# Where a second layer's hyperbolic half-steps enter, and how one formula is dealt over steps

## The chip, the cores and the metric

The kernel runs on one core of a Trainium2 chip. The metric is the time of one execution on the device in microseconds (us). The compute engines are TensorE (PE; its weight loads are a row of their own, PEld), VectorE (DVE), ScalarE (ACT) and GpSimd (POOL); SP issues most of the DMAs. Each engine works through its own queue in order, and the queues meet only at semaphores.

## The reference, cut to what matters

Two transformer layers over x of shape (4, 1024, 128), each an adaptive layer norm, an attention, a second norm and a mixture of experts. The change touches the attention of the second one ("layer 1"). It has 16 causal heads of width 8 in three groups: 6 plain, 4 hyperbolic, 6 with normalised queries and keys. The plain and normalised ones are `softmax(q k^T * scale + causal)`. The hyperbolic ones compute for each pair of positions

```
inner  = q k^T - tq * tk            # tq, tk = sqrt(1/curv + sum of squares)
arg    = max(-curv * inner, 1 + 1e-7)
dis    = sqrt(1/curv) * arccosh(arg)
scores = 1 / (eps + dis) + causal   # then softmax over keys, times v
```

## The kernel before, in words

The batches go one after another (`b` = 0 to 3), and each passes through the attention and the experts of both layers. In an attention, four heads are a *unit*. The scores are kept transposed, keys on partitions: a unit has `NS` = 12 steps, one for each chunk of 512 queries and each block of 128 keys that it sees (4 for chunk 0, 8 for chunk 1). The widths of the steps are 512, 384, 256, 128 and then five times 512, 384, 256, 128 columns a head.

Layer 1 has three standard units, so 36 standard steps, and one hyperbolic unit (`HYP_UNIT` = 3), whose 12 steps are cut into 24 *halves* of two heads (`HYP_HALVES`). Half k belongs to step k // 2. All engines walk through the same *positions* p = 0, 1, 2, ... Position p holds standard step p, and the halves enter one a position from `HYP_AT` = 2 on: half k is at position k + 2. Its work is spread over four positions (p its entry):

- p: TensorE forms the products (`hyp_scores`, L717), behind everything else of its position.
- p + 1: VectorE forms the argument and its square (`hyp_arg`, L1344 and L1349); ScalarE takes the square root by logarithm and exponential (`hyp_root`, L983 and L984); GpSimd adds root and argument (L1624).
- p + 2: ScalarE runs the rest of the score (`hyp_score`, L989, L992, L995); VectorE adds the negated maxima (`hyp_shift`, L1357).
- p + 3: ScalarE's exponential (`hyp_exp`, L1000); GpSimd's causal cut; TensorE's product with the values (`hyp_values`, L772).

In each position ScalarE first does the two exponentials of the standard step (`std_exp`, L1011), then `hyp_exp`, `hyp_score` and `hyp_root` of three different halves. VectorE does the outputs that are due, `hyp_arg`, the first half of its side jobs, `hyp_shift`, the second half of them.

Score products, standard and hyperbolic, share two pairs of PSUM banks in turn (`take_banks`, with the order written out in `JOBS`): each waits until the one two before it has been read.

Softmax needs row maxima before the scores. They are worked out ahead by *side jobs* (`side_plan`): a `piece` is a product of queries and keys in the other orientation (L628, with the causal mask added by L631) in one of two side banks, reduced by VectorE (L1284). `maxima` gathers the pieces of a unit, `max` transposes the result (L635, L637) and SP sends it on as a row. For the hyperbolic unit a maximum goes through the same formula as a score first. This is done for each chunk of queries alone, by turns on VectorE and ScalarE (L1242 to L1250, L970 to L978, `hyp_max`), and the row is spread through DRAM (`spread_hyp_maxima`). Chunk 0's is done ahead of position 0. Chunk 1's pieces lie in positions 0 to 4, the whole formula in position 4, the row in 6. The pieces of unit 1 lie in 6 to 9, those of unit 2 in 13 to 21. Other side jobs are `turn` (an output is transposed and divided) and, near the end, the first norm of the next batch.

Of the kernel before, what the change touches and what calls it, by code (L numbers as in the profile page):

```python
# [9 lines left out]
NT = N // P  # L10
# [76 lines left out]
HYP_AT = 2  # L87
HYP_HALVES = 2 * NS

# [5 lines left out]
POSITIONS = (UNITS * NS, max(3 * NS, HYP_AT + HYP_HALVES + 3) + 1)  # L95
# [7 lines left out]
def score_jobs(l):  # L103

    steps = STD_UNITS[l] * NS
    jobs = [(False, 0, 0), (False, 0, 1)]
    for p in range(POSITIONS[l]):
        if p + 1 < steps:
            jobs += [(False, p + 1, 0), (False, p + 1, 1)]
        if l and 0 <= p - HYP_AT < HYP_HALVES:  # L110
            jobs.append((True, p - HYP_AT, (p - HYP_AT) % 2))
    return jobs
# [16 lines left out]
def side_plan(l, more):  # L129
# [47 lines left out]
    for p in sorted(plan):  # L177
        items = []
        for kind, what in plan[p]:
            on_pe = kind not in ("maxima", "stats0", "norm0")  # L180
# [58 lines left out]
def adaln_kernel(nc, ins, out):  # L239
    with ExitStack() as ctx:  # L240
# [300 lines left out]
        def tensor_program(pe, b):  # L541
# [18 lines left out]
            def attention(l):  # L560
# [229 lines left out]
                for p in range(POSITIONS[l] + 1):  # L790
# [5 lines left out]
                    if l and 0 <= p - HYP_AT - 3 < HYP_HALVES:  # L796
                        hyp_values(p - HYP_AT - 3)
                    for x in extra:
                        side_job(*x)
                    if l and 0 <= p - HYP_AT < HYP_HALVES:  # L800
                        hyp_scores(p - HYP_AT)
# [94 lines left out]
        def scalar_program(act, b):  # L896
# [47 lines left out]
            def attention(l):  # L944
# [21 lines left out]
                def hyp_max(c):  # L966
# [4 lines left out]
                    nc.scalar.activation(z, z, ACT.Exp, scale=0.5).then_inc(hyp_s, 1)  # L971
                    act.wait_ge(hyp_mx, 2 * c + 2)
# [42 lines left out]
                if l:  # L1015
                    hyp_max(0)
                for p in range(POSITIONS[l]):
                    if p < steps:
                        std_exp(p)
                    if l:  # L1020
                        k = p - HYP_AT
                        if 0 <= k - 3 < HYP_HALVES:
                            hyp_exp(k - 3)
                        if 0 <= k - 2 < HYP_HALVES:
                            hyp_score(k - 2)
                        if 0 <= k - 1 < HYP_HALVES:
                            hyp_root(k - 1)
                        for c in range(NC):
                            if ("maxima", None, (HYP_UNIT, (c,))) in SIDE[l, more][p]:
                                hyp_max(c)  # L1030
# [58 lines left out]
        def vector_program(dve, b):  # L1089
# [120 lines left out]
            def attention(l):  # L1210
# [6 lines left out]
                def maxima(u, chunks):  # L1217
# [21 lines left out]
                    if is_hyp(l, u):  # L1239

                        c = chunks[0]
# [3 lines left out]
                        dve.wait_ge(hyp_s, 2 * c + 1)  # L1245
# [678 lines left out]
```

## Time and profile before

| | us |
|---|---|
| median of 3 runs | 2766.61 (2758.28 to 2769.98) |
| the profiled execution | 2764.56 |
| its span, first to last instruction | 2762.6 |
| TensorE busy | 2252.7 (82%) |
| VectorE busy | 1553.4 (56%) |
| ScalarE busy | 1380.8 (50%) |
| GpSimd busy | 660.7 (24%) |

The clock that TensorE was granted had a mean of 0.81 of full speed. Layer 1's attention of batch 0 lies between about 410 and 655 us of the span; the other three batches follow at distances of some 665 us. Times in rows count from the span's start. A *step* in the text on ScalarE is the time from one standard step's first exponential to the next one's; step 0 of batch 0 begins at 413.76.

### The profile page before, as it was taken

To read this page: it belongs to the slowest core of one execution; us is meant where nothing else is said; L and a number is where in the kernel's file an instruction comes from. 1 tells how busy PE (TensorE), PEld (TensorE's weight loads), DVE (VectorE), ACT (ScalarE), POOL (GpSimd) and SP (SyncE) were. 2 spreads that over 40 slices of the span, in tenths; PEclk is the share of its full clock that TensorE was granted. 3 is DMA by queue.
4 is the path that set the end of the run, shared out by engine and by line. 5 is a ranking of instruction groups with operands and counts; after the bars stand their busy time and mean duration, and the time that the engine had idled before them with its cause. 6 is when DMAs were issued, how large, how long until landed. Compare 5 with 4: busy or idle time off the path is not lost. (4 is left out here: it accounts for less than half of the span.)

```text
span 2762.6 us, 30066 instructions
## 1 busy us (share of the span) xinstructions
PE 2252.7 (82%) x10649; PEld 861.1 (31%) x10649; DVE 1553.4 (56%) x3429; ACT 1380.8 (50%) x1963; POOL 660.7 (24%) x639
## 2 busy tenths in 40 slices
PE   3899867778999896777998987768799998677789
PEld 1222432224433242222443234122343324322234
DVE  2564466666555256675655526566655534666542
ACT  1145426894234532898324452489522454268932
POOL 1012202332422210333331120133242111023324
PEclk9599965568999995667999987566799999655689
DMA  5200230001500023100430012210061002300012
GB/s 140 53 19 2 73 81 31 18 1 48 142 23 19 2 77 92 33 2 1 121 89 23 2 37 79 55 33 1 12 151 43 19 1 77 77 31 18 1 43 88
DMA packets 67845, 128.31 MB, mean 46 GB/s; under 512 B 11396, under 2 KB 24836, under 8 KB 63076
## 3 DMA queue, kind: packets, MB, share of 16 engines
q1 hardware_dynamic: 67696, 126.40, 17.2%
q8 instruction: 84, 1.38, 0.2%
q14 instruction: 65, 0.53, 0.1%
HBM read 109.99 MB, written 15.20 MB: 45 GB/s over the span
## 5 line engine op out<-in xcount | busy, mean ns | idle before, releaser
L1284 DVE TENSOR_REDUCE mx<-ps 128x1 f32<-128x512 f32 (+3 forms) x1248 | 641.5, 553 | 461.1 <-PE ps L631 335.9
L1011 ACT ACTIVATE pr<-ps 128x1024 f32<-128x1024 f32 (+3 forms) x672 | 515.9, 804 | 457.6 <-PE ps L701 455.2
L628 PE MATMUL ps<-kop,qop 72*128 72x512 bf16 (+6 forms) x1248 | 455.7, 388 | 142.1 <-DVE mx L1284 103.9
L701 PE MATMUL ps<-qop,kop 75*128 75x512 bf16 (+7 forms) x1344 | 419.6, 379 | 92.3 <-DVE wb L1344 32.7
L1571 POOL TENSOR_SCALAR_AFFINE_SELECT pr<-pr 128x512 f32<-128x512 f32 x224 | 149.5, 668 | 951.6 <-ACT pr L1011 950.6
L747 PE MATMUL ps<-pr,vt 128*32 128x512 f32 (+3 forms) x2688 | 360.4, 615 | 7.2 <-POOL pr L1571 6.1
L1068 ACT ACTIVATE pr<-ps 128x512 f32<-128x512 f32 x224 | 133.8, 597 | 344.1 <-PE ps L854 280.5
L628 PEld LDWEIGHTS ps<-kop,qop 72*128 72x128 bf16 (+1 forms) x1248 | 124.6, 103 | 551.0 <-DVE mx L1284 329.4
L701 PEld LDWEIGHTS ps<-qop,kop 75*128 75x128 bf16 (+1 forms) x1344 | 125.1, 107 | 328.6 <-ACT pr L1011 127.2
L631 PE MATMUL ps<-maskqk,identb 128*128 128x128 bf16 x832 | 202.3, 251 | 0.0
L864 PE MATMUL ps<-pr,w_down 128*128 128x512 f32 x384 | 197.7, 600 | 3.1 <-POOL pr L1562 3.1
L851 PE MATMUL ps<-hT,w_gate 128*128 128x512 f32 x384 | 196.1, 592 | 0.2 <-DVE on L1509 0.2
L754 PE MATMUL ps<-pr,ones 128*32 128x512 f32 (+3 forms) x1536 | 167.3, 508 | 0.0
L1334 DVE COPY osb<-ps 128x512 f32<-128x512 f32 x64 | 44.1, 689 | 213.6 <-PE ps L754 176.0
L1562 POOL TENSOR_TENSOR pr<-on,wb 128x512 f32<-128x512 f32 x84 | 106.3, 1265 | 142.3 <-DVE on L1509 130.9
L854 PE MATMUL ps<-hT,w_up 128*128 128x512 f32 x256 | 130.7, 592 | 0.0
L1344 DVE TENSOR_SCALAR wb<-ps 128x1024 f32<-128x1024 f32 (+3 forms) x96 | 91.7, 955 | 66.2 <-PE ps L717 65.4
L717 PE MATMUL ps<-qop,kop 84*128 84x512 bf16 (+3 forms) x192 | 69.4, 457 | 66.2 <-ACT pr L1011 66.1
L1624 POOL TENSOR_TENSOR wb<-wb 128x1024 f32<-128x1024 f32 (+3 forms) x36 | 72.4, 2010 | 174.1 <-ACT wb L984 174.1
L851 PEld LDWEIGHTS ps<-hT,w_gate 128*128 128x128 f32 x384 | 72.2, 190 | 88.8 <-issue 73.2
L631 PEld LDWEIGHTS ps<-maskqk,identb 128*128 128x128 bf16 x832 | 90.1, 108 | 30.8 <-issue 24.2
L1509 DVE TENSOR_TENSOR on<-pr,ps 128x512 f32<-128x512 f32 x84 | 57.4, 683 | 64.2 <-ACT pr L1068 63.8
(298 smaller groups left out, 3001.8 us busy)
## 6 DMA issues: line engine op xcount, KB each, us to landing
wb<-gates_scratch SPq DMA_DIRECT2D x192, 256.0 KB, 3.3
kop<-kparts_scratch SPq DMA_DIRECT2D x32, 576.0 KB
qop<-qparts_scratch SPq DMA_DIRECT2D x96, 192.0 KB
on<-hmax_scratch SPq DMA_DIRECT2D x8, 1024.0 KB, 5.3
kparts_scratch<-on SPq DMA_DIRECT2D x12, 256.0 KB, 2.9
qparts_scratch<-on SPq DMA_DIRECT2D x12, 256.0 KB, 4.7
qparts_scratch<-wb SPq DMA_DIRECT2D x12, 256.0 KB, 2.9
kparts_scratch<-wb SPq DMA_DIRECT2D x12, 256.0 KB, 2.8
```

The lines of the kernel that those rows point to most:

```text
L628: mm = pe.matmul(o, qop[0:k, slot(l, u), j, qb * P:(qb + 1) * P], kop[0:k, slot(l, u), j, k0:k0 + wd], start=True, stop=not diag)
L631: mm = pe.matmul(o[:, wd - P:wd], identb[:], maskqk[:], start=False, stop=True)
L701: mm = pe.matmul(o, kop[0:k, slot(l, u), 2 * pair + j, kb * P:(kb + 1) * P], qop[0:k, slot(l, u), 2 * pair + j, q0:q0 + wd], start=True, s ...
L747: mm = pe.matmul(ps[32 * j:32 * j + 32, 4, o0:o0 + wd], vt[:, kb, 32 * h:32 * h + 32], pr[:, g % 3, j, o0:o0 + wd], start=kb == 0, stop=la ...
L754: mm = pe.matmul(ps[32 * j:32 * j + 32, 5, o0:o0 + wd], ones32[:], pr[:, g % 3, j, o0:o0 + wd], start=kb == 0, stop=last, tile_position=(0 ...
L851: mm = pe.matmul(ps[:, f.gate_banks[i % R], :], wt, h, start=True, stop=True)
L854: mm = pe.matmul(ps[:, 4 + i % 2, :], wt, h, start=True, stop=True)
L864: pe.matmul(ps[:, c, :], wt, fh[:, i % 3, :], start=i < NC, stop=i == f.last[c]).then_inc(g.down, 1)
L1011: nc.scalar.activation(pr[:, g % 3, 2 * pair:2 * pair + 2, o0:o0 + wd], ps[:, bank:bank + 2, o0:o0 + wd], ACT.Exp).then_inc(a.exps, 1)
L1068: nc.scalar.activation(fa[:, i % 3, :], ps[:, f.gate_banks[i % R], :], fn).then_inc(g.act, 1)
L1284: ins_ = nc.vector.tensor_reduce(mx[:, nth(l, u) % 2, j, qb, col % 2:col % 2 + 1], ps[:, bank, 0:wd], AX.X, ALU.max, negate=True)
L1571: nc.gpsimd.affine_select(past, past, [[0, 4], [1, P]], ALU.is_ge, 0.0, base=0, channel_multiplier=-1).then_inc(at[l].cut, 1)
```

## The change

The halves enter at the positions of a list, three of every four from 1 on (1, 2, 3, 5, 6, 7, 9, ... 30, 31), and `hyp_at(p)` tells which half, if any, enters at p. All engines ask it in the place of `p - HYP_AT`. The order inside a position stays. Chunk 0's row of hyperbolic maxima moves from position 1 to 0. Chunk 1's pieces lie in 0 to 5, and its formula is cut in three: gathering, argument, square and ScalarE's root in position 5, the sum and ScalarE's remaining activations in 7, the sign in 8, the row in 9. The share of side jobs that VectorE does ahead of its shift is rounded down and not up, and where there is no shift all stand together. The outputs of the hyperbolic unit fall to the new positions.

```diff
-HYP_AT = 2
 HYP_HALVES = 2 * NS
+HYP_POS = [1 + 4 * k // 3 for k in range(HYP_HALVES)]
+NOBODY = -1
+def hyp_at(p):
+    return HYP_POS.index(p) if p in HYP_POS else NOBODY
...
-        outs += [(HYP_AT + 2 * (4 + 8 * c) + 3, HYP_UNIT, c) for c in range(NC)]
+        outs += [(HYP_POS[2 * (4 + 8 * c) - 1] + 4, HYP_UNIT, c) for c in range(NC)]
...
-        plan[1].append(("max", (HYP_UNIT, (0,))))
-        pieces(HYP_UNIT, 0, 4, (1,))
-        plan[6].append(("max", (HYP_UNIT, (1,))))
+        plan[0].append(("max", (HYP_UNIT, (0,))))
+        pieces(HYP_UNIT, 0, 5, (1,))
         pieces(1, 6, 9)
+        plan[7].append(("maxima1", (HYP_UNIT, (1,))))
+        plan[8].append(("maxima2", (HYP_UNIT, (1,))))
+        plan[9].append(("max", (HYP_UNIT, (1,))))
...
 # ScalarE, in each position
-                        k = p - HYP_AT
-                        if 0 <= k - 3 < HYP_HALVES:
-                            hyp_exp(k - 3)
+                        if hyp_at(p - 3) != NOBODY:
+                            hyp_exp(hyp_at(p - 3))
...
+                        if ("maxima", None, (HYP_UNIT, (1,))) in SIDE[l, more][p]:
+                            hyp_max_root(1)
+                        if ("maxima1", None, (HYP_UNIT, (1,))) in SIDE[l, more][p]:
+                            hyp_max(1)
...
 # VectorE
+                def hyp_maxima_sum(c):
+                    z = of_hyp(nr[:, 0, :], c)
+                    dve.wait_ge(hyp_s, 2 * c + 1)
+                    nc.vector.tensor_tensor(z, z, of_hyp(nr[:, 1, :], c), ALU.add).then_inc(hyp_mx, 1)
+                def hyp_maxima_sign(c):
+                    dve.wait_ge(hyp_s, 2 * c + 2)
...
+                    shift = hyp_at(p - 2) if l else NOBODY
+                    if l and hyp_at(p - 1) != NOBODY:
+                        hyp_arg(hyp_at(p - 1))
+                    first = len(SIDE[l, more][p]) // 2 if shift != NOBODY else 99
```

## Rows read from the trace of the kernel before

**Rows 1.** The page, part 1: busy us, share of the span, instructions.
```profile
PE 2252.7 (82%) x10649; PEld 861.1 (31%) x10649; DVE 1553.4 (56%) x3429; ACT 1380.8 (50%) x1963; POOL 660.7 (24%) x639
```
**Rows 2.** Busy time by stretch, batch 0: steps 0-3, 4-12, 13-22, 23-34, all.
```profile
core 0: us, PE busy (x) PEld busy (x) DVE busy (x) ACT busy (x) POOL busy (x), PEclk, DMA share, GB/s
413.76:437.65 23.89, 20.44 (x89) 6.18 (x89) 15.47 (x28) 7.51 (x11) 2.54 (x4) 0.57 0.12 46
437.65:511.43 73.78, 52.97 (x216) 14.05 (x214) 47.31 (x81) 59.98 (x89) 22.37 (x22) 0.62 0.11 31
511.43:602.76 91.33, 72.96 (x273) 21.53 (x273) 63.65 (x101) 80.07 (x91) 30.41 (x18) 0.59 0.00 1
602.76:644.45 41.69, 33.72 (x202) 13.05 (x200) 22.67 (x69) 36.55 (x64) 14.11 (x19) 0.80 0.01 2
413.76:644.45 230.69, 180.09 (x776) 54.80 (x776) 149.11 (x279) 184.11 (x252) 69.43 (x63) 0.64 0.05 15
```
**Rows 3.** Timeline (start us, us, what): starts of steps 18 and 19.
```profile
559.72 1.00 ACT L1011 ACTIVATE pr<-ps 128x1024 f32<-128x1024 f32 x1
...
568.20 1.92 ACT L1011 ACTIVATE pr<-ps 128x1024 f32<-128x1024 f32 x2
```
**Rows 4.** Groups of ScalarE's instructions by shape, batch 0's stage.
```profile
L992 ACT ACTIVATE wb<-wb,consts,hyp 128x512 f32<-128x512 f32 x8 | 6.1, 807 | 0.1
...
L984 ACT ACTIVATE wb<-wb 128x1024 f32<-128x1024 f32 x4 | 4.2, 1057 | 0.1
...
L984 ACT ACTIVATE wb<-wb 128x768 f32<-128x768 f32 x3 | 2.5, 843 | 0.1
...
L984 ACT ACTIVATE wb<-wb 128x512 f32<-128x512 f32 x1 | 0.6, 630 | 0.0
...
L984 ACT ACTIVATE wb<-wb 128x256 f32<-128x256 f32 x1 | 0.4, 417 | 0.0
```
**Rows 5.** Timeline, step 15: the way of a half to its root.
```profile
530.19 0.64 ACT L1011 ACTIVATE pr<-ps 128x256 f32<-128x256 f32 x2
...
534.30 1.06 PE L717 MATMUL ps<-qop,kop 84*128 84x512 bf16 x2
...
535.47 1.23 DVE L1344 TENSOR_SCALAR wb<-ps 128x1024 f32<-128x1024 f32 x1
...
536.73 1.23 DVE L1349 SCALAR_TENSOR_TENSOR rsb<-wb 128x1024 f32<-128x1024 f32 x1
...
537.87 2.08 DVE L1284 TENSOR_REDUCE mx<-ps 128x1 f32<-128x512 f32 x3
537.99 1.06 ACT L983 ACTIVATE rsb<-rsb 128x1024 f32<-128x1024 f32 x1 [0.99 <-DVE rsb L1349]
```
**Rows 6.** Timeline: GpSimd's sum twice.
```profile
540.21 3.08 POOL L1624 TENSOR_TENSOR rsb<-rsb,wb 128x1024 f32<-128x1024 f32 x1 [6.45 <-ACT rsb L984]
...
568.37 2.36 POOL L1624 TENSOR_TENSOR hT<-hT,wb 128x1024 f32<-128x1024 f32 x1 [6.13 <-ACT hT L984]
```
**Rows 7.** Timeline: the first root of batch 0.
```profile
435.60 1.06 ACT L983 ACTIVATE hT<-hT 128x1024 f32<-128x1024 f32 x1 [6.62 <-DVE hT L1349]
```
**Rows 8.** Timeline: steps 4 and 5 and the formula between.
```profile
437.65 1.92 ACT L1011 ACTIVATE pr<-ps 128x1024 f32<-128x1024 f32 x2
...
448.93 0.22 ACT L970 ACTIVATE nr<-nr 128x16 f32<-128x16 f32 x1 [2.90 <-DVE nr L1243]
...
451.36 1.92 ACT L1011 ACTIVATE pr<-ps 128x1024 f32<-128x1024 f32 x2
```
**Rows 9.** Timeline: steps 29 and 30 of batch 0, then of batch 1.
```profile
629.98 1.94 ACT L1011 ACTIVATE pr<-ps 128x1024 f32<-128x1024 f32 x2
...
632.24 1.94 ACT L1011 ACTIVATE pr<-ps 128x1024 f32<-128x1024 f32 x2 [0.32 <-PE ps L701]
...
1290.61 1.02 ACT L1011 ACTIVATE pr<-ps 128x1024 f32<-128x1024 f32 x1
...
1295.57 1.94 ACT L1011 ACTIVATE pr<-ps 128x1024 f32<-128x1024 f32 x2 [2.24 <-PE ps L701]
```
**Rows 10.** Timeline: the products of the last output.
```profile
648.15 0.48 DVE L1319 TENSOR_TENSOR kT<-ps,rec 128x32 f32<-128x32 f32 x4
```

More of the change, by code:

```diff
@@ L94 @@
 STD_UNITS = (UNITS, UNITS - 1)
[L95 removed]
+POSITIONS = (UNITS * NS, max(3 * NS, HYP_POS[-1] + 4) + 1)
 def nth(l, u):
@@ L109, in score_jobs @@
             jobs += [(False, p + 1, 0), (False, p + 1, 1)]
-        if l and 0 <= p - HYP_AT < HYP_HALVES:
-            jobs.append((True, p - HYP_AT, (p - HYP_AT) % 2))
+        if l and hyp_at(p) != NOBODY:
+            jobs.append((True, hyp_at(p), hyp_at(p) % 2))
     return jobs
@@ L179, in side_plan @@
         for kind, what in plan[p]:
-            on_pe = kind not in ("maxima", "stats0", "norm0")
+            on_pe = kind not in ("maxima", "maxima1", "maxima2", "stats0", "norm0")
             items.append((kind, n if on_pe else None, what))
@@ L795, in attention @@
                         values(p, extra)
-                    if l and 0 <= p - HYP_AT - 3 < HYP_HALVES:
-                        hyp_values(p - HYP_AT - 3)
+                    if l and hyp_at(p - 3) != NOBODY:
+                        hyp_values(hyp_at(p - 3))
                     for x in extra:
                         side_job(*x)
-                    if l and 0 <= p - HYP_AT < HYP_HALVES:
-                        hyp_scores(p - HYP_AT)
+                    if l and hyp_at(p) != NOBODY:
+                        hyp_scores(hyp_at(p))
                 if l:
@@ L1015, in attention @@
                 if l:
+                    hyp_max_root(0)
                     hyp_max(0)
@@ L1244, in maxima @@
                                                        op1=ALU.mult).then_inc(hyp_mx, 1)
[L1245 to L1250 removed]
+                        if chunks[0] == 0:
+                            hyp_maxima_sum(0)
+                            hyp_maxima_sign(0)
                         return
@@ L1255, in maxima, with of_hyp @@
                     split(m, lambda k: of(nmp[:, 32 * k:32 * k + 32]), x).then_inc(a.nmp, 1)
+                def of_hyp(t, c):
+                    return t.rearrange("p (j q) -> p j q", q=NT)[:, :, 4 * c:4 * c + 4]
+                def hyp_maxima_sum(c):
[4 more added lines that the diff above has]
+                    dve.wait_ge(hyp_s, 2 * c + 2)
+                    if c:
+                        dve.wait_ge(a.side, count("max", (HYP_UNIT, (0,))))
+                    nc.vector.tensor_scalar(of_hyp(nm[:, nth(l, HYP_UNIT) % 2, :], c), of_hyp(nr[:, 0, :], c), -1.0,
+                                            None, ALU.mult).then_inc(a.nmp, 1)
                 def side_job(kind, g, what):
@@ L1259, in side_job @@
                         maxima(*what)
+                        return
+                    if kind == "maxima1":
+                        hyp_maxima_sum(1)
+                        return
+                    if kind == "maxima2":
+                        hyp_maxima_sign(1)
                         return
@@ L1374, in attention @@
                             outputs_out(i)
-                    k = p - HYP_AT
-                    if l and 0 <= k - 1 < HYP_HALVES:
-                        hyp_arg(k - 1)
-                    first = (len(SIDE[l, more][p]) + 1) // 2 if l and k >= 0 else 99
+                    shift = hyp_at(p - 2) if l else NOBODY
+                    if l and hyp_at(p - 1) != NOBODY:
+                        hyp_arg(hyp_at(p - 1))
+                    first = len(SIDE[l, more][p]) // 2 if shift != NOBODY else 99
                     for x in SIDE[l, more][p][:first]:
                         side_job(*x)
-                    if l and 0 <= k - 2 < HYP_HALVES:
-                        hyp_shift(k - 2)
+                    if shift != NOBODY:
+                        hyp_shift(shift)
                     for x in SIDE[l, more][p][first:]:
```

32 lines of the change are left out of this document (13 added, 19 removed).

## The prediction

> **What bounds the kernel now.** The chain of waits only reaches back from the end of the last feed-forward block, so I read the engines' totals first and then stages. TensorE is busy 82% of the span, but at a mean clock of 0.81 and with pipelined matmuls, so that row names no bound [rows 1]. The diff touches only layer 1's attention, which runs four times, once a batch. I cut batch 0's at the starts of ScalarE's standard exponentials, the first thing ScalarE does in each step: steps 0 to 3 take 23.9 us, 4 to 12 73.8, 13 to 22 91.3 and 23 to 34 41.7, 230.7 in all [rows 2]. ScalarE is busy 7.5, 60.0, 80.1 and 36.6 of these. From step 4 on it is busy over 80% and the other engines less: it is the bound of the stage wherever hyperbolic halves run, and its idle time (16.4 + 13.8 + 11.2 + 5.1 = 46.5 us a batch) is all that a new order can win. The change takes nothing from its work.
>
> ScalarE's work in a step is, in this order: two standard exponentials, then the exponential of the half that entered three steps ago, the score chain (four kinds of line, L989 to L995) of the one of two steps ago, and the square root (L983, L984) of the one before. At full width a step without a wait lasts 568.20 - 559.72 = 8.48 us [rows 3]. From the durations [rows 4], start to start, that is 1.8 standard + 0.95 exponential + 3.7 score + 2.0 root. The L984 rows scale the last three with width: 1.06, 0.84, 0.63, 0.42 us for 512, 384, 256, 128 columns a head, so a score is 3.7, 2.9, 2.35, 1.8 and a root 2.0, 1.6, 1.2, 0.8 (the last two score figures hold fixed costs, an estimate between the L984 and L992 rows).
>
> **Part 1: the halves enter at positions 1, 2, 3, 5, 6, 7, 9, ... 31 and not at 2 to 25.** ScalarE's work by range follows from which halves fall in it. Steps 0 to 3 gain root 1 and score 0: 7.5 + 5.7 = 13.2. Steps 4 to 12 lose scores 0 and 8, roots 1 and 9 and exponential 7: 60.0 - 11.8 = 48.2. Steps 13 to 22 gain score 8, root 9, exponential 7 and lose scores 15 to 18, roots 16 to 19, exponentials 15 to 17: 80.1 - 18.0 = 62.1. Steps 23 on get the sum of these, 36.6 + 24.1 = 60.7. So the long tail of 41.7 us, where only standard steps run at 2 to 3 us, is filled, and the middle is thinned. What decides is the waits.
>
> A thinned step loses its filling. In the present order, between the exponentials and the root stands always a score chain (3.7 us), which hides the way of a new half: product on TensorE (L717), argument and square on VectorE (L1344, L1349), root. In step 15 the exponentials began at 530.19, the product at 534.30, the argument at 535.47, the square ended at 537.96 and the root began at 537.99 after a wait of 0.99 us: 7.8 us of way under a cover of about 6.5 [rows 5]. With a gap every fourth position, the second step after it (6, 10, 14, ... 30) has a root but no score: the cover is 1.8 + 0.95 = 2.8 us. Say step 18 begins at T, when the score chain of step 17 ends. VectorE then adds the maxima (L1357) until T + 1.2, has half of step 17's side jobs left (three reductions of 0.69, L1284), and TensorE issues the fifth piece only after the first of them, at T + 2.6, then the product (1.06) until 3.7, argument and square (1.23 each) until 6.25. The root waits 6.25 - 2.8 = 3.4 us. Bounds: 1.9 if nothing but the exponential's bank holds the product (T + 4.7), 5.0 by the 7.8 of rows 5; less than 1.9 is not possible while the queue orders stand. I take 3.4, because TensorE has less queued in front of that product than in step 15. By width and by what stands in the side list (the maxima of unit 2 lie in 21, those of unit 1 in 9): step 10 3.2, step 14 3.6, step 18 3.4, step 22 5.4; step 6 1.1 (it is masked by the wait of part 2), step 26 2.0, step 30 0.5. VectorE's and TensorE's queues behind these waits hold nothing that the next step wants sooner.
>
> The step after it (7, 11, ... 31) has a score directly after its standard exponentials, and that score needs GpSimd's sum (L1624), 2.36 us from the root's end [rows 6]. Today an exponential lies between. Behind a standard step of 128 columns (steps 15 and 23) this costs 2.5 - 0.75 = 1.7 us, at 27 1.1, at 19 0.5. Bounds 0 and 2.4; that GpSimd's sum can last 3.08 [rows 6] is in the unnamed waits below. The Trainium skill (SBUF — State Buffer, section "Who interferes with whom") says that VectorE with two SBUF inputs and a GpSimd operation that reads SBUF take turns at one port pair. The 3.08 against 2.36 agrees. By this rule the thinner middle meets fewer such clashes, which would take up to 0.7 us off a sum; I leave the sum as it is.
>
> The start: half 0's product comes at TensorE's position 1 and not 2. Now the first root begins at 435.60 after 6.62 us without work [rows 7]. VectorE in steps 2 and 3 gets argument and square before the pieces (2.46 each) and one shift, against one or two reductions fewer a step. Walking it through, the first root begins near 429.5, sum and score end at 437.8, the second root at 439.9, where step 4 begins, 2.2 us later than now (437.65). Bounds -3 (the fewer pieces win) and +5 (all added VectorE work, 6.1 us, less one reduction).
>
> **Part 2: the second maxima's formula over three steps.** Now it stands in step 4: ScalarE waits 2.90 us for VectorE (L970), and its small activations with the waits between them fill the time to 451.36; step 4 takes 13.7 us against 8.5 [rows 8]. The work stays. VectorE no longer waits in place for ScalarE. Not ScalarE's: its root of the formula waits in position 5 for VectorE's maxima of the same position, which stand last in the list and behind the shift (which waits for ScalarE's score of that step): shift 0.95 + two reductions 1.3 + three small operations and links 1.0 = 3.3 us after the score. The second part waits in position 7 for VectorE's sum of position 7, again last behind shift and three reductions: 1.5 us beyond the root. Bounds 0 (VectorE is ahead) and 5 together with rows 8's larger wait. That the maxima's row goes out at position 9 and not 6 costs nothing: it is first read at 13. Moving the first row from position 1 to 0 gives half 0 its maxima in time. I put it at nothing: its formula ends before ScalarE's step 0, which TensorE's position 0 waits for anyway; it costs up to 1 us if it does not. SP's order is the same.
>
> **Part 3: the tail.** The hyperbolic output of the second chunk now leaves one position before the last standard one, so its reciprocal, four products (0.48) [rows 10] and four transposes join the end: I take +0.9 us, between 0.5 (the products alone) and 1.5.
>
> **Sum for a batch.** Steps 0 to 3: +2.2. Steps 4 to 12: 48.2 + waits 3.3 + 1.5 + 1.1 + 3.2 + 1.0 unnamed = 58.3, against 73.8: -15.5. Steps 13 to 22: 62.1 + 14.6 named + 3.0 unnamed = 79.7, against 91.3: -11.6. Steps 23 to 34: 60.7 + 5.9 named (1.7 + 1.1 + 2.0 + 0.5 and 0.6 at the last two) + 2.5 unnamed = 69.0, against 41.7: +27.3. Tail +0.9. Together +3.3 us; four batches +13. The unnamed waits are those of today's middle (11.2 in ten steps), scaled down because every third of them is now named or gone. The profiled execution took 2764.6 us (span 2762.6 and 2.0 around it), 2.0 less than the median of the runs, 2766.6. So 2778 in its terms and **2780 us** in the median's, 0.5% over.
>
> **Rivals.** A, the tail runs at 1.2 GHz (2800): now the clock is 0.80 in steps 23 to 34 and 0.59 in 13 to 22 [rows 2], and one standard step of the tail that met the low clock in batch 1 took 4.96 us (1290.61 to 1295.57, 2.24 of wait for TensorE), where batch 0's took 2.26 (629.98 to 632.24) [rows 9]. If two such steps a batch fall into low clock beyond what I have, that is 2 x 2.7 x 4 = +22. For it: with halves in the tail ScalarE paces TensorE. Against it: at ScalarE's 5 us a step the low clock mostly still suffices. The Trainium skill (TensorE: Matmul & The Clock Gate, section "What's actually happening") says that half rate is the default and sustained activity lifts it. By that rule the tail turns slow; the two clocks of rows 2 agree.
>
> B, faster (2735): the root's way is shorter than its cover needs. If VectorE's second half of side jobs is through before the score ends, the waits of steps 10 to 22 fall to the bound of 1.9 or less (-7 us), and if it is also early for the formula, the 4.8 us of part 2 go: 3.3 - 11.8 = -8.5 a batch, -34. For it: VectorE is busy only 64 of 91 us in steps 13 to 22 [rows 2]. Against it: its shift stands in order before those jobs and waits for ScalarE. It decides from 3.3 us of waits less a batch; the place to look is steps 10, 14, 18, 22.
>
> C, no difference (2766): waits of today's middle vanish with the thinner load and outweigh the new ones by just the cost of the tail.
>
> **Chances.** Forecast 0.45, of which 0.17 within 0.5% (about what a measurement of this kernel can tell from no change); A 0.15; B 0.30; C 0.10. Faster by over 0.5%: 0.30; within: 0.27; slower: 0.43. The likeliest case alone spans 2766 to 2798. The whole range takes B's price and A's with some of the start's +5 (x 4 = +11 over +2.2): 2732 to 2812.
>
> **What would show it.** In the changed profile: ScalarE's busy time in the stage the same within 2 us; step 13 beginning 11 to 16 us earlier after step 0 and step 23 20 to 30 earlier; L983 with waits of 2 to 5 us on VectorE's L1349 in steps 10, 14, 18 and 22; L989 waiting on GpSimd's sum; L970 (the formula) still waiting 2 us or more; steps 23 to 34 at 65 us or more. It is wrong if L983's waits stay near 1 us, if the middle gains over 35 us, or if the tail takes under 60.

## The result, and the profile after

The changed kernel takes 2825.39 us (median of 4 runs, 2823.14 to 2828.78), beside 2764.91 (2758.28 to 2769.98) for the kernel before in the same session: a ratio of 1.0212, 95% interval 1.0185 to 1.0239. The forecast was 2780, 2732 to 2812. The direction was right, and the time lies 13 us above the range. One of the ten runs of e2 below, 2924.73 us at a granted clock of 0.72, was a slow one and is left out of its ratio; the median listed for e2 holds it and would be 2761.65 without it.

The page's part 1 of the kernel after answers to [rows 1]: no engine has more work.

```profile
PE 2234.1 (79%) x10649; PEld 854.1 (30%) x10649; DVE 1540.6 (55%) x3429; ACT 1377.4 (49%) x1963; POOL 654.3 (23%) x639
```

Busy time by stretch, batch 0 of the kernel after, cut as in [rows 2]:

```profile
core 0: us, PE busy (x) PEld busy (x) DVE busy (x) ACT busy (x) POOL busy (x), PEclk, DMA share, GB/s
413.18:439.83 26.65, 21.43 (x86) 6.15 (x87) 17.71 (x29) 13.03 (x17) 4.85 (x5) 0.50 0.12 40
439.83:507.50 67.67, 47.47 (x212) 13.36 (x212) 39.01 (x77) 48.07 (x76) 16.96 (x19) 0.68 0.11 29
507.50:590.55 83.05, 61.53 (x259) 18.62 (x259) 54.57 (x93) 61.98 (x71) 20.77 (x14) 0.64 0.02 5
590.55:659.90 69.35, 45.66 (x212) 13.65 (x212) 34.65 (x75) 59.94 (x91) 23.42 (x24) 0.68 0.00 1
413.18:659.90 246.72, 176.09 (x768) 51.77 (x768) 145.93 (x273) 183.02 (x252) 66.00 (x62) 0.65 0.05 14
```

ScalarE is busy 183.0 us against 184.1; its idle time rose from 46.6 to 63.7. The means over the four batches, each cut in the same way, are the safer measure of the lengths:

| steps | before | after | difference | forecast |
|---|---|---|---|---|
| 0 to 3 | 24.0 | 25.5 | +1.5 | +2.2 |
| 4 to 12 | 72.7 | 67.4 | -5.3 | **-15.5** |
| 13 to 22 | 89.8 | 81.9 | -7.9 | -11.6 |
| 23 to 34 | 42.9 | 68.4 | +25.5 | +27.3 |
| all | 229.4 | 243.2 | +13.8 | +2.4, and 0.9 for the tail |

Four times 13.8 is 55 of the 58.6 us between the two profiled executions (2764.56 and 2823.14); the other 3.4 leave 0.8 a batch for everything else, the end of the stage among it, for which 0.9 was forecast. What ScalarE waited for in batch 0's stage after the change (us in total, times, longest):

```profile
ACT wb L995 <- DVE wb L1381: 11.5, 6, 4.5
ACT hT L995 <- DVE hT L1381: 11.0, 3, 6.6
ACT pr L1023 <- PE ps L709: 8.9, 4, 4.2
ACT rsb L995 <- DVE rsb L1381: 4.6, 1, 4.6
ACT wb L1001 <- POOL wb L1656: 4.0, 3, 1.9
ACT hT L1001 <- POOL hT L1656: 3.8, 2, 1.9
ACT nr L985 <- DVE nr L1273: 3.3, 1, 3.3
...
ACT nr L978 <- DVE nr L1255: 2.9, 1, 2.9
```

L995 is the root, L1381 the square, L1001 the first line of the score, L1656 GpSimd's sum, L978 and L985 the two parts of the formula, L1023 the standard exponential. Most of these are waits that the forecast named. The timeline below has four of steps 4 to 12: the one of step 5, which the forecast had about right (3.3), and three that it had too small or not at all, two in step 7 and one before step 12:

```profile
456.71 0.21 ACT L978 ACTIVATE nr<-nr 128x16 f32<-128x16 f32 x1 [2.92 <-DVE nr L1255]
...
470.08 0.63 ACT L995 ACTIVATE wb<-wb 128x512 f32<-128x512 f32 x1 [2.24 <-DVE wb L1381]
...
474.72 0.31 ACT L985 ACTIVATE nr<-nr,consts 128x16 f32<-128x16 f32 x1 [3.34 <-DVE nr L1273]
...
500.50 1.94 ACT L1023 ACTIVATE pr<-ps 128x1024 f32<-128x1024 f32 x2 [3.89 <-PE ps L709]
```

### The profile page after: what moved, and what is told of

Its sections match the earlier page's. It is cut to its first block and busy times, and to the rows that moved or that the text cites. A ratio compares the mean times of both kernels' runs of the same rounds, so it can differ in the third digit from the quotient of the medians.

```text
span 2820.3 us, 30066 instructions
## 1 busy us (share of the span) xinstructions
PE 2234.1 (79%) x10649; PEld 854.1 (30%) x10649; DVE 1540.6 (55%) x3429; ACT 1377.4 (49%) x1963; POOL 654.3 (23%) x639
## 5 line engine op out<-in xcount | busy, mean ns | idle before, releaser
L1023 ACT ACTIVATE pr<-ps 128x1024 f32<-128x1024 f32 (+3 forms) x672 | 514.3, 804 | 424.0 <-PE ps L709 421.8
L636 PE MATMUL ps<-kop,qop 72*128 72x512 bf16 (+6 forms) x1248 | 444.0, 378 | 139.3 <-DVE mx L1316 93.6
L709 PE MATMUL ps<-qop,kop 75*128 75x512 bf16 (+7 forms) x1344 | 419.3, 376 | 126.7 <-ACT pr L1023 46.3
L725 PE MATMUL ps<-qop,kop 84*128 84x512 bf16 (+3 forms) x192 | 64.6, 429 | 108.1 <-ACT pr L1023 108.1
L1656 POOL TENSOR_TENSOR wb<-wb 128x1024 f32<-128x1024 f32 (+3 forms) x36 | 70.1, 1946 | 166.4 <-ACT wb L996 166.4
L755 PEld LDWEIGHTS ps<-pr,vt 128*32 128x32 f32 x2688 | 57.7, 117 | 115.9 <-issue 81.6
```

Source lines behind the costliest of these rows:

```text
L636: mm = pe.matmul(o, qop[0:k, slot(l, u), j, qb * P:(qb + 1) * P], kop[0:k, slot(l, u), j, k0:k0 + wd], start=True, stop=not diag)
L709: mm = pe.matmul(o, kop[0:k, slot(l, u), 2 * pair + j, kb * P:(kb + 1) * P], qop[0:k, slot(l, u), 2 * pair + j, q0:q0 + wd], start=True, s ...
L755: mm = pe.matmul(ps[32 * j:32 * j + 32, 4, o0:o0 + wd], vt[:, kb, 32 * h:32 * h + 32], pr[:, g % 3, j, o0:o0 + wd], start=kb == 0, stop=la ...
L1023: nc.scalar.activation(pr[:, g % 3, 2 * pair:2 * pair + 2, o0:o0 + wd], ps[:, bank:bank + 2, o0:o0 + wd], ACT.Exp).then_inc(a.exps, 1)
```

## Experiments

All ratios are to the kernel before on the same chip. Ranges of steps are means over the four batches.

### Is it the gaps or the formula (e1 to e4)

```diff
 # e1: chunk 1's formula whole in position 5
-        plan[7].append(("maxima1", (HYP_UNIT, (1,))))
-        plan[8].append(("maxima2", (HYP_UNIT, (1,))))
 # and ScalarE's hyp_max, VectorE's sum and sign follow at once in position 5
...
 # e2 / e3 / e4, in the changed kernel
-HYP_POS = [1 + 4 * k // 3 for k in range(HYP_HALVES)]
+HYP_POS = [2 + k for k in range(HYP_HALVES)]           # e2
+HYP_POS = [1 + k for k in range(HYP_HALVES)]           # e3
+HYP_POS = [1 + 8 * k // 7 for k in range(HYP_HALVES)]  # e4: three gaps
```

> The changed kernel with its second maxima's formula whole in position 5 (gathering, root, sum, remaining activations and sign one after another, as in the kernel before), everything else as changed. Theory G (the empty positions cost: a root that has no score chain as its cover, a score that waits for GpSimd's sum): the formula is a side matter, 2825 us become 2815 to 2830. Theory F (the dealt formula costs: in the changed kernel ScalarE waits 2.9 us in step 5 and 3.3 us in step 7 for it, and step 7 takes 13.8 us): the second wait goes and step 7 falls to 9 or 10 us, so 3 to 4 us a batch, 2810 to 2815, but with theory F as the main cause 2785 or less.

> The changed kernel with the halves entering one a position from 2 on, as before (position = 2 + k); the dealt formula and the rounding of the side jobs stay. Theory G: the loss goes whole, 2755 to 2775 us, no wait of the root (logarithm line of hyp_root) above 1.5 us from step 13 on. Theory F: a good part of it stays, 2790 or more.

> The changed kernel with the halves entering one a position from 1 on (1 + k), without gaps; the rest as changed. Theory G: near the kernel with positions from 2, 2750 to 2775 us, as only the gaps cost. Theory S (the early entry costs, as VectorE has argument, square and pieces at once in the first steps): steps 0 to 4 longer by 5 us or more a batch, 2785 or more.

> The changed kernel with one empty position in eight (1 + 8k // 7, three gaps) and not one in four (seven). Theory G: the cost goes with the number of gaps, so three sevenths of the way from the kernel without gaps to 2825 us: about 2790 (2780 to 2800), with a root wait of 3 to 5 us in the second step after each gap. A theory in which the longer stretch costs (the tail at a low clock) and not the gaps: within 5 us of the kernel without gaps, as only three positions are added.

| | us | ratio, interval | 4 to 12 | 13 to 22 | 23 to 34 |
|---|---|---|---|---|---|
| e1 | 2812.35 | 1.0162, 1.0139 to 1.0184 | 64.7 | 82.5 | 68.4 |
| e2 | 2762.6 | 0.9974, 0.9955 to 0.9993 | 75.0 | 87.0 | 46.3 |
| e3 | 2761.9 | 0.9967, 0.9946 to 0.9989 | 76.2 | 85.4 | 40.5 |
| e4 | 2780.85 | 1.0045, 1.0025 to 1.0065 | 71.1 | 85.3 | 49.6 |

Without gaps (e3) the rest of the change costs nothing; seven gaps cost 63.5 us (2825.4 - 2761.9) and three cost 19, less than three sevenths of it. The early entry is free: e2 and e3 are alike. Dealing the formula is no gain where there are gaps: whole (e1) it is 13 us faster, theory F's smaller price. The main cost is theory G's, the gaps.

(A gap is a position at which no half enters.) What the gaps cost ScalarE can be read from its waits. The means a batch over steps 0 to 34, in the kernel after and in e3, are: for a root 28.9 and 12.9 us, for GpSimd's sum 8.8 and 4.9, for the exponential that begins step 12 3.7 and none, for the other standard exponentials 4.7 and 10.2, for the formula 5.6 and 6.8. So uncovered roots and sums cost 19.9 us more a batch, and the tail, where halves fill waits for TensorE, gives 5.5 back. The 3.7 us before step 12 (15 in four batches) have a cause of their own, which e15 takes away. The 63.5 us are therefore not the price of missing cover alone.

### What holds a root that no score covers (e5, e9)

```diff
 # e5, VectorE: all side jobs ahead of the shift before such a root
-                    first = len(SIDE[l, more][p]) // 2 if shift != NOBODY else 99
+                    first = len(SIDE[l, more][p]) // 2 if shift != NOBODY and p % 4 != 1 else 99
 # e9, TensorE: the product ahead of the older half's and of the side jobs
+                    early = l and p % 4 == 1 and p != 5 and hyp_at(p) != NOBODY
+                    if early:
+                        hyp_scores(hyp_at(p))
                     if l and hyp_at(p - 3) != NOBODY:
                         hyp_values(hyp_at(p - 3))
...
-                    if l and hyp_at(p) != NOBODY:
+                    if l and hyp_at(p) != NOBODY and not early:
                         hyp_scores(hyp_at(p))
```

> The changed kernel, with VectorE doing all side jobs of positions 1, 5, 9, ... ahead of its shift. These are the positions before a root that no score chain covers. Theory V (the uncovered root waits because half of the side jobs stand between VectorE's shift and the argument): steps 14, 18 and 22 get shorter by 1.3 to 2 us each, steps 10 to 22 by some 5 us a batch, total near 2805 (2798 to 2815). Rival P (the product on TensorE, held by banks and by pieces, sets the root's time, whatever VectorE does first): the waits of steps 14, 18 and 22 stay at 3.7 to 4.6 us and the total at 2825 within 5. A third way (the exponential of the next position now waits for the later shift): steps 14, 18, 22 no shorter or longer, total 2825 to 2840.

> The changed kernel, with TensorE's product of a half directly behind the products with the values of the standard step, ahead of those of the older half and of the side jobs, in positions 1, 9, 13, 17, 21, 25 and 29. In batch 0 of the changed kernel the product began 3.3 us into step 14 and 4.1 us into step 18, at a low clock behind TensorE's own work, and so it did with VectorE's jobs ahead of the shift (4.1 us into step 18 to the hundredth). Theory P (in steps 14 and 18 TensorE's own queue holds the half, in 22 VectorE's): the product begins 1.1 us into the step, when the first exponential has freed its banks; steps 14 and 18 become 2 to 2.5 us shorter, step 10 about 1, step 22 stays at 8.3. Total 2825 - 4 x 4.5 to 6 = 2801 to 2807. Theory V (VectorE's jobs hold it): steps 14 and 18 less than 0.7 us shorter, total 2818 to 2828.

e5 took 2819.56 us (1.0199, 1.0177 to 1.0220), e9 2851.26 (1.0306, 1.0270 to 1.0343). Step 18 of the kernel after, from its timeline:

```profile
548.83 1.92 ACT L1023 ACTIVATE pr<-ps 128x1024 f32<-128x1024 f32 x2
...
550.50 1.92 PE L780 MATMUL ps<-hT,vt 128*32 128x512 f32 x4
...
552.97 0.74 PE L725 MATMUL ps<-qop,kop 84*128 84x512 bf16 x2
...
553.82 1.23 DVE L1376 TENSOR_SCALAR wb<-ps 128x1024 f32<-128x1024 f32 x1 [0.17 <-PE ps L725]
...
556.34 1.06 ACT L995 ACTIVATE rsb<-rsb 128x1024 f32<-128x1024 f32 x1 [4.64 <-DVE rsb L1381]
```

The same step of e5:

```profile
551.60 1.92 ACT L1023 ACTIVATE pr<-ps 128x1024 f32<-128x1024 f32 x2
...
555.74 0.64 PE L725 MATMUL ps<-qop,kop 84*128 84x512 bf16 x2
...
557.58 1.06 ACT L1012 ACTIVATE xn<-xn 128x1024 f32<-128x1024 f32 x1 [4.06 <-DVE xn L1389]
...
559.97 1.06 ACT L995 ACTIVATE rsb<-rsb 128x1024 f32<-128x1024 f32 x1 [1.34 <-DVE rsb L1381]
```

The product (L725) starts 4.14 us into the step in both, to the hundredth: VectorE's order doesn't move it. It stands behind TensorE's values of the older half (L780, 1.92 us) and the pieces. The late shift then makes the exponential wait 4.06 us instead. So theory V fell, and beside rival P the third way that e5's expectation named is what happened. Steps 13 to 22 take 1.0 us more in the mean; the 5.8 us by which e5 is faster than the kernel after lie elsewhere, among them step 25 (6.4 us for 8.4), where a wait for the next batch's norm goes. The time lies just under the ranges of both P and the third way. Step 14 of e9 shows what the earlier product does:

```profile
512.66 1.07 ACT L1026 ACTIVATE pr<-ps 128x512 f32<-128x512 f32 x2
...
513.30 1.03 PE L725 MATMUL ps<-qop,kop 84*128 84x512 bf16 x2 [1.65 <-ACT pr L1026]
...
515.27 0.29 DVE L1319 TENSOR_REDUCE mx<-ps 128x1 f32<-128x128 f32 x1 [4.73 <-PE ps L639]
515.47 1.22 DVE L1392 TENSOR_TENSOR wb<-wb,on 128x1024 f32<-128x1024 f32 x1
...
516.73 1.06 ACT L1015 ACTIVATE wb<-wb 128x1024 f32<-128x1024 f32 x1 [3.00 <-DVE wb L1392]
...
519.82 1.21 DVE L1379 TENSOR_SCALAR wb<-ps 128x1024 f32<-128x1024 f32 x1
```

The product starts 0.6 us into the step, even earlier than theory P said, but TensorE stood for its banks, the pieces came later, and VectorE's reductions, shift (L1392) and at last the argument (L1379) with them: the argument starts 7.2 us into the step, in the kernel after 4.6. Step 14 takes 11.7 us for 8.9 in the mean, step 18 9.8 for 8.9, step 22 9.4 for 8.3. Neither theory, each of which looks at one queue alone, gives e9's time: P said 2801 to 2807, V 2818 to 2828. TensorE's pieces and VectorE's reductions hand each other two banks in turn, and the half passes between them; a move in one queue comes back through the other.

### The way itself or the side jobs (e12, e13)

```diff
 # TensorE and VectorE, in a side job of kind "piece"
+                        wd = 32 if l == 1 and not is_hyp(l, u) else wd
```

e12 is the kernel after with this, e13 is e3 with it. Both leave out part of the work: the maxima of units 1 and 2 are taken over 32 keys of each piece, and the products that add the causal mask to a piece (L631 in the kernel before) are gone for these units, 48 a batch. So, unlike what the expectation says, the number of instructions is not the same.

> The changed kernel, with the pieces of the maxima of layer 1's two standard units cut to 32 columns, on TensorE and in VectorE's reductions (so these maxima are taken over part of the keys). The order and number of instructions stay. Theory J (the root that no score chain covers waits for the position's side jobs, which TensorE and VectorE hand to each other through two banks): in steps 14, 18 and 22 the root's waits of 4.6, 4.6 and 3.7 us fall to 1 to 2, and the difference to the next kernel is 20 to 40 us, where with whole pieces it is 2825.4 - 2761.9 = 63.5. Rival W (the way of the half itself, product, argument and square, is what is too long for the cover): the waits stay over 3 us and the difference at 50 to 65.

> The same cut of the pieces in the kernel whose halves enter one a position at 1 to 24, with the change's formula (2761.9 us with whole pieces). Theory J: ScalarE is near its limit there already and hides these pieces, so this kernel gains less than the one before it: total 2735 to 2750. Rival W: both gain the same.

e12 took 2792.1 us (1.0091, 1.0062 to 1.0120), e13 2724.2 (0.9841, 0.9811 to 0.9870). Steps 13 to 22 of batch 0, e12:

```profile
503.74:580.12 76.38, 48.18 (x227) 15.07 (x227) 38.74 (x93) 61.74 (x71) 20.71 (x14) 0.61 0.02 5
```

and e13:

```profile
505.97:586.67 80.70, 55.65 (x241) 15.64 (x241) 45.52 (x101) 77.24 (x91) 28.43 (x19) 0.65 0.00 1
```

The roots' waits fell (step 14 from 4.55 to 3.25, step 18 from 4.64 to 1.97, step 22 from 3.71 to 2.82), which is part of what theory J said: 12.9 us became 8.0, where J had 3 to 6. But the difference between the two kernels is 67.9 us, with whole pieces 63.5: rival W by the time. (The wait before step 12 is in both differences, 3.7 and 4.0 us a batch.) Thin pieces give both 33 to 38 us. With gaps ScalarE still idles 14.6 of the 76.4 us, without them 3.5 of 80.7. So side jobs lengthen a root's wait, but they cost the kernel without gaps as much, and what a gap costs stays with thin pieces. That it stays because the cover is missing agrees with this and with the waits above; no run gave a gap its cover back. The waits of e12's steps 4 to 22 of batch 0:

```profile
ACT wb L997 <- DVE wb L1384: 6.1, 4, 3.2
ACT pr L1025 <- PE ps L711: 5.1, 1, 5.1
...
ACT hT L997 <- DVE hT L1384: 2.8, 1, 2.8
...
ACT xn L997 <- DVE xn L1384: 2.0, 1, 2.0
ACT rsb L997 <- DVE rsb L1384: 2.0, 1, 2.0
```

### The formula asked for one position later (e6, e7, e8)

```diff
 # ScalarE
-                        if ("maxima", None, (HYP_UNIT, (1,))) in SIDE[l, more][p]:
+                        if ("maxima", None, (HYP_UNIT, (1,))) in SIDE[l, more][p - 1]:
                             hyp_max_root(1)
-                        if ("maxima1", None, (HYP_UNIT, (1,))) in SIDE[l, more][p]:
+                        if ("maxima1", None, (HYP_UNIT, (1,))) in SIDE[l, more][p - 1]:
                             hyp_max(1)
-        plan[8].append(("maxima2", (HYP_UNIT, (1,))))
+        plan[9].insert(0, ("maxima2", (HYP_UNIT, (1,))))
```

e6 is the kernel after with this, e7 is e2 and e8 is e3 with it.

> The changed kernel, with ScalarE's two parts of the second maxima's formula one position later each (root at the end of position 6, the rest at the end of 8; VectorE's sum stays in 7) and the sign first in position 9. Theory F (the dealt formula costs because ScalarE asks in the same position in which VectorE forms its input last): the waits of 2.92 us in step 5 and 3.34 us in step 7 go, and the late root of step 7 (2.24) in part; the sum of VectorE in 7 is not late. Steps 4 to 12 become 60 to 63 us for 67.7, the total 2825 - 4 x 5 to 7 = 2797 to 2805. Rival (these waits were cover for the roots' way, which is then late by as much): total 2818 to 2828, with the waits moved to the roots of steps 6 to 8.

> As the run before it, but the halves enter at positions 2 to 25, one a position, as in the kernel before. That kernel order with the formula asked for in its own position took 2762.6 us with a step 7 of 15.1 us. Theory F: step 7 falls to about 10 us, and the total to 2762.6 - 4 x 4 to 6 = 2738 to 2747, 1% below the kernel before. Rival (ScalarE is not alone at its limit there, VectorE and TensorE need the time): total 2755 to 2765.

> As the run before it, but the halves enter at positions 1 to 24. With the formula asked for in its own position this order took 2761.9 us with a step 7 of 15.0 and a step 5 of 10.2 us. Theory F: both fall to 9 to 10, total 2735 to 2747, 1% below the kernel before. Rival: 2755 to 2765.

| | us | ratio, interval | step 5 | step 7 |
|---|---|---|---|---|
| e6 | 2809.26 | 1.0157, 1.0129 to 1.0185 | 5.8 (9.2 after) | 8.4 (13.6) |
| e7 | 2726.74 | 0.9865, 0.9841 to 0.9890 | 8.1 | 7.9 (15.7 in e2) |
| e8 | 2722.90 | 0.9856, 0.9827 to 0.9885 | 7.4 (10.2 in e3) | 8.1 (15.0) |

Without gaps theory F holds, and its price was too small (35.9 and 39.0 us won, 15 to 27 expected). With them it is half right: 16.1 us for 20 to 28, a time between F's and the rival's. The formula's waits (2.92 and 3.34 in batch 0) go, but the roots of steps 6 and 10 now wait 2.39 and 4.70 us for 1.32 and 2.42, and that of step 7 2.20 as before. So the formula's waits had been cover for roots, as the rival said.

### The product earlier in every position (e10, e11)

```diff
 # TensorE, in e8
+                    if l and hyp_at(p) != NOBODY:
+                        hyp_scores(hyp_at(p))        # e10 here
                     if l and hyp_at(p - 3) != NOBODY:
                         hyp_values(hyp_at(p - 3))
+                                                     # e11 here
                     for x in extra:
                         side_job(*x)
-                    if l and hyp_at(p) != NOBODY:
-                        hyp_scores(hyp_at(p))
```

> Halves at positions 1 to 24, the formula's ScalarE parts one position later (2722.9 us), and TensorE's product of a half directly behind the products with the values of the standard step, in every position. There ScalarE waits 3.4 us for the root of step 10, 1.8 in step 7, 2.6 and 0.7 in step 14, 1.1 in 15. Theory P: the root's waits of steps 7, 10 and 15 go, total 2722.9 - 4 x 3 to 5 = 2703 to 2711. Rival: TensorE now stands before the product until the exponential has freed its banks, up to 1 us a step, and its side jobs come late to VectorE: total 2725 to 2745.

> As the run before it, but the product stands behind the products of the older half with its values and ahead of the side jobs. TensorE seldom stands for the banks then. Theory P: total 2705 to 2715. Rival: the side jobs come late to VectorE and with them its shift: total 2722 to 2735.

e10 took 2830.29 us (1.0239, 1.0206 to 1.0271), e11 2775.32 (1.0036, 1.0013 to 1.0059), 107 and 52 more than e8: the rivals' direction, far beyond their price. ScalarE's waits for roots rise from 13.3 us a batch in e8 to 33.2 and 23.5. VectorE's waits for pieces in batch 0's stage, e8:

```profile
DVE mx L1316 <- PE ps L639: 22.4, 19, 3.2
...
DVE mx L1316 <- PE ps L636: 7.7, 9, 2.0
```

and e10:

```profile
DVE mx L1319 <- PE ps L639: 40.2, 21, 6.5
DVE mx L1319 <- PE ps L636: 21.2, 10, 3.7
```

In e10 TensorE stands for the exponential's banks (21.9 us in this stage for 13.7 in e8) with the pieces behind it, and VectorE gets them late: 61.4 us of waits for 30.1. In e11 VectorE's waits for pieces are 51.5 us, but TensorE waits for the exponential's banks no longer than in e8 (13.1). There it is its next standard products that wait for VectorE to read the half before (18.6 us for 11.6). Which of the two holds the pieces in e11 was not tested.

### The row and the spread ahead of it (e15, e16, e17), and the shift (e14)

```diff
 # e15, SP, inside spread_hyp_maxima(c), behind the store of hrow
+                if c:
+                    send_maxima(1, b + 1 < B, 1, BOTH)
                 sp.wait_ge(hm_stored, 16 * (c + 1))
 # and at the end of the loop over c
-            send_maxima(1, b + 1 < B, 1, BOTH)
 # e14, VectorE, in e8
-                    first = len(SIDE[l, more][p]) // 2 if shift != NOBODY else 99
+                    first = min(len(SIDE[l, more][p]) // 2, 1) if shift != NOBODY else 99
```

e16 is e14 with e15's edit, e17 is e6 with it.

> The changed kernel, in which SP sends the maxima row of unit 1 (three DMAs of 8 KB) before it spreads the second hyperbolic row over 128 partitions (1024 KB) and not behind it. In the changed kernel the row is 4.7 us on its way and TensorE waits 5.0 us for it, ScalarE then 3.9 before step 12; in the kernel before, with three positions between the two transfers, it is 1.9 and 1.2 us. Theory D (the moved spread delays the row): the row lands after 1.9 us, ScalarE's wait falls to 1 to 2, total 2825.4 - 4 x 2 to 3 = 2813 to 2817. Rival (the row comes late by its own chain, the maxima of position 9): the wait stays, 2822 to 2828.

> The same swap in the fastest order so far (2717.8 us), where TensorE waits 2.2 us for the row and ScalarE not at all. Theory D: no difference, 2714 to 2721, since ScalarE's chain is longer there. Rival (TensorE's later start reaches step 12 or 13): 2708 to 2714.

> The changed kernel with both mends together: ScalarE's parts of the formula one position later (alone 2809.3 us, 16.1 less than the changed kernel) and unit 1's row sent before the second hyperbolic row is spread (alone 2812.4, 13.0 less). Theory A (the two are separate costs of part 2): total 2825.4 - 25 to 30 = 2795 to 2800, with the gaps' own price left over. Rival (with the formula's waits gone the steps before 12 are shorter, and the wait for the row takes up what was won): 2802 to 2810.

> The fastest kernel so far (halves at 1 to 24, ScalarE's parts of the formula one position later, 2722.9 us), with at most one side job of VectorE ahead of its shift. There the exponential of step 14 waits 2.57 us for the shift, behind half of seven jobs. Theory J: that wait goes and part of it returns at the root of step 14 or 15, total 2712 to 2721. Rival (the jobs behind the shift hold the argument and so the root by as much as was won): total 2721 to 2730.

SP's issues in the kernel after, then its DMAs (KB each, us to landing), both around 490:

```profile
492.91 0.38 SPq L1747 DMA_DIRECT2D on<-hmax_scratch  x1
493.34 1.97 SPq L1731 DMA_DIRECT2D qop<-mrow  x3
```

```profile
on<-hmax_scratch SPq DMA_DIRECT2D x1, 1024.0 KB, 6.0
...
qop<-mrow SPq DMA_DIRECT2D x3, 8.0 KB, 4.7
```

In the kernel before the spread was issued 31.8 us ahead of the row:

```profile
464.66 0.38 SPq L1715 DMA_DIRECT2D on<-hmax_scratch  x1
496.44 1.83 SPq L1699 DMA_DIRECT2D qop<-mrow  x3
```

and the row landed after 1.9 us. In e15:

```profile
on<-hmax_scratch SPq DMA_DIRECT2D x1, 1024.0 KB, 5.4
...
qop<-mrow SPq DMA_DIRECT2D x3, 8.0 KB, 2.3
```

e15 took 2812.36 us (1.0156, 1.0125 to 1.0187), 13.0 less than the kernel after: theory D, just under what was expected. ScalarE's wait before step 12 fell from 3.89 to 0.53. e16 took 2719.5 (0.9816, 0.9789 to 0.9843), no different from e14, as D said. e17 took 2791.58 (1.0081, 1.0057 to 1.0105), 33.8 less than the kernel after and more than the two alone (16.1 + 13.0). Its steps 4 to 12 last 58.6 us in the mean. Batch 0:

```profile
439.49:499.27 59.78, 49.56 (x212) 14.06 (x212) 39.38 (x77) 47.79 (x76) 16.65 (x19) 0.64 0.12 34
```

e14 took **2717.79 us** (0.9822, 0.9796 to 0.9849) and has, with e16, the lowest median: 1.8% under the kernel before, and 5.1 us under e8, less than the spread of e8's own runs. With the shift ahead of all but one job step 14 falls from 11.1 to 8.3 us; step 10 rises from 8.4 to 10.3.

Why step 14 falls is more than what e14's expectation names (jobs ahead of the shift). In e8 VectorE's shift of that step begins just behind GpSimd's sum and lasts 3.33 us, where it takes 1.22 alone, and the exponential waits for it:

```profile
517.62 2.34 POOL L1656 TENSOR_TENSOR xn<-xn,wb 128x1024 f32<-128x1024 f32 x1 [5.35 <-ACT xn L996]
517.72 3.33 DVE L1389 TENSOR_TENSOR hT<-hT,on 128x1024 f32<-128x1024 f32 x1
...
521.08 1.06 ACT L1012 ACTIVATE hT<-hT 128x1024 f32<-128x1024 f32 x1 [2.57 <-DVE hT L1389]
```

In e14 the shift is over before the sum begins at 514.58:

```profile
512.56 1.22 DVE L1389 TENSOR_TENSOR hT<-hT,on 128x1024 f32<-128x1024 f32 x1 [1.78 <-ACT hT L1007]
```

In all four batches of e8 the shift of step 14 takes 3.3 us; none of e14's takes over 1.3. Of the 2.57 us of wait 2.1 are the longer shift.

## Why the prediction was wrong, and where it was right

**ScalarE's work by range: right.** 13.2, 48.2, 62.1 and 60.7 us were worked out from [rows 2, 4]; 13.0, 48.1, 62.0 and 59.9 were measured. The miss is in waits.

**The start: right.** The first root was put near 429.5 and step 4 at 2.2 us later. The timeline after, which answers to [rows 7]:

```profile
429.50 1.06 ACT L995 ACTIVATE hT<-hT 128x1024 f32<-128x1024 f32 x1 [6.57 <-DVE hT L1381]
```

Step 4 begins at 439.83. Counted from step 0 that is 2.8 us later in batch 0 and 1.5 in the mean.

**The uncovered roots: the mechanism right, the sizes near, the holder partly wrong.** Steps 6, 10, 14, 18, 22 and 26 were put at 1.1, 3.2, 3.6, 3.4, 5.4 and 2.0 us of wait; batch 0 has 1.3, 2.4, 4.6, 4.6, 3.7 and 1.5. The walk of step 18 let the product begin at 2.6 and end at 3.7 us into the step; it began at 4.1 and ended at 4.9 (in step 14 it began at 3.3), behind the older half's products with the values (1.92 us, in a stretch with a mean clock of 0.56), which the walk did not contain. e12 and e13 show that a good part of these waits stays with thin pieces. GpSimd's sum behind steps 15, 19, 23 and 27 was put at 1.7, 0.5, 1.7 and 1.1 and measured 1.9, 0.6, 1.9 and 1.4. The unnamed waits were 5.6 and 4.0 us for 3.0 and 2.5: 1.7 of them in the middle is an exponential (L1012, step 17) whose shift lasted 2.20 us and not 1.22 beside GpSimd's sum, 2.6 in the tail a wait for the next batch's norm.

**The failed step: part 2's terms in steps 4 to 12.** In the means 10.2 of the 11.4 us a batch by which the ranges missed lie there. Batch 0 has 19.6 us of waits in them (67.67 - 48.07), the sum had 10.1. The formula in step 5 is right (3.3 against 2.92). Three terms are not:

- The row. "That the maxima's row goes out at position 9 and not 6 costs nothing: it is first read at 13" looked at who reads that row and not at who stands behind it. SP sends 1024 KB 0.4 us ahead of unit 1's row, which step 12 needs at once, and ScalarE waits 3.9. Of SP the prediction says only that its order is the same: the order was, the distance was not. e15 shows it, with 13.0 us. This is the largest of the three, and it was put at nothing.
- The formula in step 7. It was put at "1.5 us beyond the root"; it took 3.34.
- The root of step 7, which the sum does not name. It waited 2.24 us. Its product began only at 467.75, 5.1 us into the step, behind five pieces and a turn of outputs. e1 and e6 have that wait too (2.6 and 2.2 us), and without gaps it is 1.8 (e3, e8) and in the kernel before 1.4, so it comes neither from the dealing nor, for the most part, from the gaps.

The rest is small: an exponential that waits 1.3 us for its shift in step 10, a root that waits 1.0 in step 12, against 1.0 that was unnamed. And 1.1 of the 10.2 us is the base: the sum was made against batch 0, whose steps 4 to 12 took 73.8 us before, the mean 72.7.

With the formula's parts a position later and the row first (e17) the kernel takes 33.8 us less, and its steps 4 to 12 take 58.6 us beside the 58.3 of the sum. That they agree is luck. The sum had 4.8 us of waits for the formula and 4.3 for the roots of steps 6 and 10; e17 has none for the formula and 9.2 for the roots of steps 6, 7 and 10 (2.39, 2.13 and 4.70) in batch 0. So the price of a root without cover in these steps was sized too low as well: the waits for the formula hid part of it, as the forecast itself said of step 6 ("masked by the wait of part 2"). The remaining 11.6 us of e17 above the forecast are the middle's: its four ranges differ from the kernel before by +0.6, -14.1, -6.9 and +25.5 us, where +2.2, -15.5, -11.6 and +27.3 were forecast, 2.7 us a batch in all and 4.7 in steps 13 to 22. There too part is the base (91.3 in batch 0, 89.8 in the mean).

Of the prediction's own signs, step 13 began 3.3 us earlier after step 0 in batch 0 and not 11 to 16, and step 23 11.6 earlier and not 20 to 30; the roots' waits, the sum's and the tail came as it said.

The Trainium skill (DMA: Bandwidth & Descriptors, section "Queues, rings and completion order") says that each DMA engine consumes the descriptors of one issuing queue in ring order. The 4.7 us behind the spread, 2.3 ahead of it and 1.9 far from it agree, but they would also with transfers that share bandwidth: the runs do not tell the two apart.

**The tail: right.** 69.35 us against 69.0. Rival A did not come: the granted clock fell from 0.80 to 0.68 there, but ScalarE waits 9.4 us in all, and for TensorE never by more than 0.2. TensorE has 202 matmuls in the 41.7 us of before and 212 in the 69.4 of after. The Trainium skill (TensorE: Matmul & The Clock Gate, section "What's actually happening") says that the lower rate is the default and that activity lifts it. The lower mean clock of a tail with its matmuls further apart agrees; it had no price here.

**Rival B did not come** in the kernel as changed. What it asked of VectorE's order (the formula early) is what e6 to e8 had to build; the roots' waits of steps 14, 18 and 22 stayed at 3.3, 2.0 and 2.8 us even with thin pieces.

**GpSimd's sum.** In batch 0 three full-width sums of the middle took 2.81 to 3.08 us before, and each had met a shift of VectorE (L1357), which has two inputs in SBUF; after, none is longer than 2.36 us. By the port rule of the Trainium skill (SBUF — State Buffer, section "Who interferes with whom") such a pair takes turns. The trace agrees: four full-width sums overlapped a shift by more than 0.1 us before, one after. The prediction looked at the sum alone. Where the sum begins first it is the shift that is long: 2.60 us in step 14 before, 2.20 in step 17 after, 1.22 alone, and the exponential behind it waits 2.58 and 1.72 us.

**Open.** Why e17 gains 4.7 us more than its parts, which is near the spread of the runs; whether the landing of the row behind the spread is order or shared bandwidth; and whether a gap could be made free by giving ScalarE other work in the place of the score, which no run tried.

## What to carry to other kernels

When a pipeline's bound engine has no more work but its work is spread thinner, ask for each new hole what it covered until now: here the score chain hid the way of the next half over three engines. Each of seven holes a batch cost 1.8 us with the formula as changed (e15 against e3, 50.5 / 28) and 2.5 with its waits gone (e17 against e8, 68.7 / 28), both without the late row. When a step with a large transfer is moved, look at what is issued right behind it on the same queue, not only at who reads it. And an engine should ask for a helper's result one position after the helper forms it: that alone was worth 36 to 39 us here without holes, and 16 with them, where the waits had hidden others. A wait that goes can uncover another that it hid, so a sum of waits is no forecast of what their removal gives.

## What the runs showed of the hardware

Three DMAs of 8 KB issued 0.4 us behind one of 1024 KB on SP's queue landed after 4.7 us, after 2.3 when they were issued ahead of it (e15), and after 1.9 with nothing near.

VectorE's addition of two SBUF tensors (128x1024 f32, 1.22 us alone) and GpSimd's of the same size (2.35 alone) take turns: where GpSimd's began 0.1 us earlier, VectorE's took 3.33 us (e8, four batches of four); where VectorE's began 0.35 us earlier, GpSimd's took 3.08 (the kernel before).

Moving one product ahead of the older half's and of the side jobs in TensorE's queue, with no change of work, cost 107 us on 2723 (e10); ahead of the side jobs alone 52 (e11).
